# A fused image-and-text Mamba block: one state in four gets u times B from TensorE as a turned u times a diagonal of B, and the queues get another order

## The chip, the cores and the metric

The kernel runs on one core of a Trainium2 chip. A core has five engines with a queue each: PE (TensorE, matrix products into PSUM), DVE (VectorE), ACT (ScalarE), POOL (GpSimd) and SP (SyncE), which issues nearly all DMAs here. Each queue runs in order, and engines meet through semaphores. The metric is the device time of one execution in microseconds; the median of three runs of the kernel before is 1729.16 (1728.2 to 1730.28).

## The reference

64 images of 96x96 become 36 patch tokens each, a class token goes in front and 77 text tokens behind: 114 tokens of 256 values. A layer norm and a selective state-space layer follow, then a layer norm and a shared feed-forward part, and for 512 chosen rows a part with 8 experts. The state-space layer takes most of the time:

```
delta = softplus(dt @ W_dt + b_dt)
dA  = exp(delta[..., None] * A)
dBu = delta[..., None] * Bm[:, :, None, :] * xc[..., None]
h = dA_t * h + dBu_t
y = einsum('bdn,bn->bd', h, C_t)
```

There are 512 channels d and 16 states n; h runs over the 114 tokens of each sequence. With u = delta * xc the summand of the recurrence is u[d, t] * B[n, t].

## The kernel before

Sequences are taken in pairs, 32 groups of 228 columns (tokens). The main loop makes one step for each group, and a step also does the earlier layers for the next groups and the later layers for the groups before. In a step the 512 channels and 16 states are cut into 16 units (k = 0 to 15, UNITS): a unit holds one block of 128 channels (c = k // 4) and, on its 128 partitions, 4 states of 32 channels each, with four blocks of 32 channels side by side: 4 x 228 = 912 columns.

A unit goes through five instructions. POOL makes u times B into a ring of 8 SBUF buffers (`dbu`, line 1646, reading `bbc`, the rows of B spread over partitions). ACT writes the decays exp(delta * A) into one of two PSUM slots of 912 columns (`exps`, line 1010, four instructions). DVE runs the recurrence as a scan over both (`scan`, line 1307). The product with C is made by DVE from the slot (`times_c`, line 1316), or, for the six units of `ON_POOL`, by POOL (line 1654); for these the scan writes to the ring buffer. PE adds up the states with four matmuls on 32 rows of output each (`reduce_states`, line 711, after the skip product of line 708 at each first state of a block). The slot of a unit is free when its product, or for a unit of `ON_POOL` its scan, is done; only then may ACT fill it for the unit after next.

The order of each engine's queue is written out in the bodies of its block, as a loop over k with conditions. On ACT the window (`window`) stands behind unit 1: SiLU of the convolved x for the next group and of z, with a table load before and after (lines 1041, 1047, 1132). On PE the z projection of the next group (`proj_z`, line 610) stands behind unit 13 and the convolution (line 661) behind units 9 and 12. delta of the next group comes out behind unit 7 on DVE (line 1357), after three softplus instructions of ACT (lines 1058 to 1066); u follows on POOL (line 1667). Both go through DRAM to be spread over partitions.

## Time and profile before

| | |
|---|---|
| median of 3 runs | 1729.16 us |
| span of the profiled execution | 1726.7 us (2.5 us less than the median) |
| busy: PE, DVE, ACT, POOL | 1480.7, 1555.7, 1331.9, 1564.6 us |
| one step in the middle of the run | 49.2 us |
| mean granted TensorE clock | 0.947 of 2.4 GHz |

Busy times are those of a whole execution and hide that each stage has its own limit. PE's busy time counts a matmul until its modelled end, so back-to-back matmuls overlap; an fp32 matmul shows as two records (line 711: 4 matmuls, 8 records), a transpose as one. In the timelines the text in brackets is idle time of that engine just before the instruction, and what ended it.

### The profile page before, as it was taken

To read this page: it belongs to the slowest core of one execution; us is meant where nothing else is said; L and a number is where in the kernel's file an instruction comes from. 1 tells how busy PE (TensorE), PEld (TensorE's weight loads), DVE (VectorE), ACT (ScalarE), POOL (GpSimd) and SP (SyncE) were. 2 spreads that over 40 slices of the span, in tenths; PEclk is the share of its full clock that TensorE was granted. 3 is DMA by queue.
4 is the path that set the end of the run, shared out by engine and by line. 5 is a ranking of instruction groups with operands and counts; after the bars stand their busy time and mean duration, and the time that the engine had idled before them with its cause. 6 is when DMAs were issued, how large, how long until landed. Compare 5 with 4: busy or idle time off the path is not lost.

```text
span 1726.7 us, 28038 instructions
## 1 busy us (share of the span) xinstructions
PE 1480.7 (86%) x9868; PEld 1065.4 (62%) x9868; DVE 1555.7 (90%) x1389; ACT 1331.9 (77%) x3100; POOL 1564.6 (91%) x782
## 2 busy tenths in 40 slices
PE   7778898889888988898889889888889898977688
PEld 7555666666666666666666666666666666654355
DVE  2599999999999999999999999999999999999944
ACT  2577788888888888888888888888888888886644
POOL 0699999999999999999999999999999999999814
PEclk9888999999999999999999999999999999997899
DMA  4667755555656655656666555566665555656110
GB/s 141 138 135 180 163 130 123 122 131 132 145 129 146 132 123 122 131 130 146 129 146 135 122 125 126 130 146 129 145 138 121 125 126 129 142 119 141 36 34 15
DMA packets 194430, 218.47 MB, mean 127 GB/s; under 512 B 94011, under 2 KB 184773, under 8 KB 193778
## 3 DMA queue, kind: packets, MB, share of 16 engines
q1 hardware_dynamic: 193522, 215.51, 56.6%
q8 instruction: 78, 1.28, 0.3%
q0 software_dynamic: 576, 1.17, 0.3%
q14 instruction: 62, 0.51, 0.1%
q10 hardware_dynamic: 192, 0.01, 0.0%
HBM read 169.92 MB, written 47.09 MB: 126 GB/s over the span
## 4 chain that ended last, share of the span: by engine, by line
DVE 41%; ACT 18%; issue 16%; PE 13%; POOL 10%; DMA 2%; SPq 0%; DVEq 0%; ACTq 0%; POOLq 0%
DVE psum L1307 20%; DVE xr L1307 16%; ACT psum L1010 6%; POOL xr L1646 6%; POOL xr L1654 3%; PE psum L610 3%; DVE xr L1316 3%; ACT L1132 2%; PE psum L697 2%; PE psum L782 2%; ACT L1041 2%; ACT soft L1062 2%; ACT soft L1066 2%; ACT soft L1058 2%; PE psum L783 1%
## 5 line engine op out<-in xcount | busy, mean ns | idle before, releaser
L1646 POOL TENSOR_TENSOR xr<-u,bbc 128x912 f32<-128x912 f32 x512 | 1075.5, 2133 | 14.3 <-DMA u<-u_scratch 13.9
L1010 ACT ACTIVATE psum<-delta,a_neg 128x228 f32<-128x228 f32 x2048 | 805.9, 441 | 221.6 <-DVE xr L1316 191.2
L1307 DVE TENSOR_TENSOR_SCAN psum<-psum,xr 128x912 f32<-128x912 f32 x320 | 656.2, 2051 | 68.5 <-ACT psum L1010 59.8
L1654 POOL TENSOR_TENSOR xr<-xr,cbc 128x912 f32<-128x912 f32 x192 | 409.2, 2131 | 31.9 <-DVE xr L1307 28.5
L1307 DVE TENSOR_TENSOR_SCAN xr<-psum,xr 128x912 f32<-128x912 f32 x192 | 392.3, 2043 | 0.0
L1316 DVE TENSOR_TENSOR xr<-psum,cbc 128x912 f32<-128x912 f32 x320 | 353.7, 1105 | 11.1
L711 PE MATMUL psum<-xr,fold 128*32 128x228 f32 x4096 | 295.1, 385 | 50.6 <-POOL xr L1654 26.7
L610 PE MATMUL psum<-xh,win 128*128 128x228 f32 x1024 | 222.7, 367 | 61.8 <-ACT xs L1041 33.4
L610 PEld LDWEIGHTS psum<-xh,win 128*128 128x128 f32 x1024 | 192.1, 193 | 91.7 <-ACT xs L1041 44.0
L661 PE MATMUL psum<-xi,conv_d 128*128 128x228 f32 x1024 | 210.9, 358 | 0.0
L711 PEld LDWEIGHTS psum<-xr,fold 128*32 128x32 f32 x4096 | 96.9, 112 | 178.1 <-issue 79.4
L661 PEld LDWEIGHTS psum<-xi,conv_d 128*128 128x128 f32 x1024 | 190.2, 188 | 16.2 <-issue 11.7
L730 PE MATMUL psum<-wout,y 128*114 128x256 f32 x512 | 134.8, 411 | 0.0
L708 PE MATMUL psum<-xs,skip_w 128*128 128x228 f32 x256 | 83.2, 408 | 30.0 <-DVE y L1324 30.0
L730 PEld LDWEIGHTS psum<-wout,y 128*114 128x114 f32 x512 | 97.4, 200 | 18.8
L625 PE MATMUL psum<-xp,tokw 128*128 128x72 f32 x768 | 92.3, 278 | 8.4 <-DMA xp<-x_patches 8.4
L625 PEld LDWEIGHTS psum<-xp,tokw 128*128 128x128 f32 x768 | 92.8, 196 | 10.0 <-DMA xp<-x_patches 8.9
L1667 POOL TENSOR_TENSOR u<-delta,xs 128x912 f32<-128x912 f32 x31 | 65.9, 2125 | 18.4 <-issue 12.0
L708 PEld LDWEIGHTS psum<-xs,skip_w 128*128 128x128 f32 x256 | 40.9, 194 | 67.1 <-DVE y L1324 44.4
L697 PE MATMUL psum<-dbl,wdt 17*128 17x228 f32 x256 | 58.7, 369 | 22.2 <-ACT ob L1122 21.8
L697 PEld LDWEIGHTS psum<-dbl,wdt 17*128 17x128 f32 x256 | 46.0, 189 | 36.6 <-issue 34.0
L756 PE MATMUL psum<-x2t,w 128*128 128x228 f32 x256 | 58.8, 374 | 1.9
(204 smaller groups left out, 1574.7 us busy)
## 6 DMA issues: line engine op xcount, KB each, us to landing
delta<-delta_scratch SPq DMA_DIRECT2D x256, 228.0 KB, 6.5
u<-u_scratch SPq DMA_DIRECT2D x256, 228.0 KB, 4.2
bbc<-bc_scratch SPq DMA_DIRECT2D x128, 114.0 KB, 2.6
u_scratch<-u SPq DMA_DIRECT2D x64, 228.0 KB, 4.9
cbc<-bc_scratch SPq DMA_DIRECT2D x128, 114.0 KB, 2.7
delta_scratch<-delta SPq DMA_DIRECT2D x64, 226.0 KB, 5.7
out<-ob SPq DMA_DIRECT2D x32, 228.0 KB
h_scratch<-h SPq DMA_DIRECT2D x31, 228.0 KB
```

Source lines behind the costliest of these rows:

```text
L610: mm = pe.matmul(bank[:, c], win[:, k, at + c * P:at + (c + 1) * P], xh[:, p, k], start=(k == 0), stop=(k == DC - 1))
L625: mm = pe.matmul(tok_ps[:, c, g % 2:g % 2 + count].rearrange("p h t -> p (h t)"), tokw[:, k, c * P:(c + 1) * P], xp[:, k, g % 2:g % 2 + co ...
L661: mm = pe.matmul(conv_bank(half)[:, c].rearrange("p (s t) -> p s t", s=SEQ), conv_d[:, at, t], xi[:, at, :, t:t + T], start=(t == 0), stop ...
L697: mm = pe.matmul(dt_bank(half)[:, c], wdt[32:33 + R, (2 * half + c) * P:(2 * half + c + 1) * P], dbl[32:33 + R, :], start=True, stop=True)
L708: pe.matmul(y_ps, skip_w[:, c], xs[:, i % 2, c], start=True, stop=False)
L711: mm = pe.matmul(y_ps[j * DQ:(j + 1) * DQ], fold[:], xr[:, k % XRING, j], start=False, stop=(n == NI - 1))
L730: mm = pe.matmul(h2_ps[:, s], y[:, g % 2, c, s * T:(s + 1) * T], wout[:, c], start=False, stop=(c == CH - 1))
L1010: ins = nc.scalar.activation(slot(k)[:, j * TOK:(j + 1) * TOK], delta4[:, c // 2, j, c % 2], ACT.Exp, scale=a_neg[:, c, j, n:n + 1])
L1307: nc.vector.tensor_tensor_scan(x if k in ON_POOL else slot(k), slot(k), x, 0.0, ALU.mult, ALU.add).then_inc(scan_done, 1)
L1316: nc.vector.tensor_tensor(xr[:, k % XRING], slot(k).rearrange("p (j t) -> p j t", j=J), cbc[:, p, k % NI].unsqueeze(1).to_broadcast([P, J, ...
L1646: nc.gpsimd.tensor_tensor(xr[:, k % XRING], u4[:, c // 2, :, c % 2], bbc[:, p, n].unsqueeze(1).to_broadcast([P, J, TOK]), ALU.mult).then_i ...
L1654: nc.gpsimd.tensor_tensor(xr[:, k % XRING], xr[:, k % XRING], cbc[:, p, k % NI].unsqueeze(1).to_broadcast([P, J, TOK]), ALU.mult).then_inc ...
```

## The change

In units 0, 4, 8 and 12 (`turned(k)`: state 0 of each four) the summand u times B comes from PE and no longer from POOL. PE turns u of the whole group (`turn_u`, eight transposes into the PSUM space of slot 0), ACT copies it to SBUF (`ut_copy`), and for each turned unit `times_b` multiplies turned u with a diagonal matrix that has B of one state and sequence on its diagonal; the result goes into the unit's PSUM slot, where the decays used to be, and the decays of that unit go to the ring buffer in SBUF. The diagonal matrices lie in DRAM as zeros; two DMAs a step write B into the diagonal word by word (`diag_keep`), one reads the whole matrix back (`diag_load`). POOL makes the products with C of eight units, DVE of eight. The queues' orders are written out anew, instruction by instruction. `e1` shares the space of `win` and is loaded near the end; `est` shares that of `ut`.

```diff
-ON_POOL = (1, 3, 8, 10, 12, 14)
+TURNED = 0
+ON_POOL = ((0, 3, 5, 7, 8, 10, 12, 13),)
...
+            ut_ps = flat[0:T, 0:CH * SEQ * P].rearrange("p (c s d) -> p c s d", c=CH, s=SEQ)
...
+            def slot_free(e, i, k):
+
+                back = (k - SLOTS) % UNITS
+                step = i if k >= SLOTS else i - 1
+                if step < 0 or back in on_pool(step):
+                    need(e, scan_done, UNITS * i + k - SLOTS + 1)
+                else:
+                    e.wait_ge(c_dve, dve_products(step, back) + 1)
...
+                    def diag_keep(g):
+
+                        need(sp, diag_in, 16 * (g - 1))
+                        if g == 0:
+                            sp.wait_ge(diag_out, 32)
+                        lines = diag_scratch[g % 2].rearrange("(t x) -> t x", t=T)[:, 0:SEQ * NQ * T]
+                        spots = lines.rearrange("t (s q z) -> q s t z", s=SEQ, q=NQ)[:, :, :, 0]
+                        for s in range(SEQ):
+                            sp.dma_start(spots[:, s], dbl[TURNED:NS:NI, s * T:(s + 1) * T],
+                                         allow_slow_non_contiguous=True).then_inc(diag_out, 16)
+
+                    def diag_load(g):
+                        sp.wait_ge(diag_out, 16 * SEQ * (g + 2))
+                        need(sp, bu_mm, CH * (g - 1))
+                        sp.dma_start(diag[0:T, g % 2].rearrange("p s q t -> p (s q t)"), diag_flat(g)).then_inc(diag_in, 16)
...
                             sp.wait_ge(dbl_ev, i + 2)
                             sp.dma_start(bc_scratch[p], dbl[0:2 * NS, :]).then_inc(bc_out, 16)
+                            diag_keep(i + 1)
 
                             sp.wait_ge(bc_out, 16 * (i + 2))
-                            rows_out(bbc, p, 0, b_in)
+                            b_rows_out(p)
                             rows_out(cbc, p, NS, c_in)
+                            diag_load(i + 1)
...
+                    def turn_u(g):
+
+                        pe.wait_ge(u_done, 2 * g + 2)
+                        slot_free(pe, g, TURNED)
+                        for c in range(CH):
+                            for s in range(SEQ):
+                                mm = pe.transpose(ut_ps[:, c, s], u[:, c, s * T:(s + 1) * T], ident[:])
+                        mm.then_inc(ut_mm, 1)
+
+                    def times_b(i, k):
+
+                        c = k // NI
+                        pe.wait_ge(ut_ev, i + 1)
+                        pe.wait_ge(diag_in, 16 * (i + 1))
+                        slot_free(pe, i, k)
+                        lo = (k % SLOTS) * 1024
+                        for j in range(J):
+                            for s in range(SEQ):
+                                a = lo + j * TOK + s * T
+                                cut = min(T, 512 - a % 512)
+                                for x, z in ((0, cut), (cut, T)):
+                                    for q in range(NQ):
+                                        if x < z:
+                                            mm = pe.matmul(flat[q * DQ:(q + 1) * DQ, a + x:a + z], ut[0:T, c, s, j * DQ:(j + 1) * DQ],
+                                                           diag[0:T, i % 2, s, q, x:z], start=True, stop=True)
+                        mm.then_inc(bu_mm, 1)
...
+                        if runs(i + 1):
+                            turn_u(i + 1)
+                        if runs(i + 2):
+                            convolve(i + 2, 1)
+                        if runs(i):
+                            reduce_states(i, 12)
+                        if runs(i + 1):
+                            times_b(i + 1, 0)
...
+                        if turned(k):
+                            need(act, red_mm, v - XRING + 1)
+                            to = xr[:, k % XRING].rearrange("p j t -> p (j t)")
                         else:
-                            need(act, c_dve, N_DVE * step + ON_DVE.index(back) + 1)
+                            slot_free(act, i, k)
+                            to = slot(k)
...
+                    def ut_copy(g):
+                        act.wait_ge(ut_mm, g + 1)
+                        need(act, bu_mm, CH * g)
+                        nc.scalar.activation(ut[0:T], ut_ps, ACT.Copy).then_inc(ut_ev, 1)
...
-                        dve.wait_ge(dbu_done, v + 1)
                         x = xr[:, k % XRING].rearrange("p j t -> p (j t)")
-                        nc.vector.tensor_tensor_scan(x if k in ON_POOL else slot(k), slot(k), x, 0.0,
+                        decay, added = slot(k), x
+                        if turned(k):
+                            dve.wait_ge(bu_mm, CH * i + k // NI + 1)
+                            decay, added = x, slot(k)
+                        else:
+                            dve.wait_ge(dbu_done, made(i, k) + 1)
+                        nc.vector.tensor_tensor_scan(x if k in on_pool(i) else slot(k), decay, added, 0.0,
                                                      ALU.mult, ALU.add).then_inc(scan_done, 1)
...
+                        if turned(k):
+                            return
                         need(pool, red_mm, v - XRING + 1)
```

On PE the end of a step and the start of the next read so before, from the feed-forward input (L756) over the convolution (L661), the state reductions (L711, eight for two units) and the z projections (L610):

```order
L756 MATMUL psum<-x2t,w 128x228 x4
L661 MATMUL psum<-xi,conv_d 128x228 x8
L711 MATMUL psum<-xr,fold 32x228 x8
L708 MATMUL psum<-xs,skip_w 128x228
L711 MATMUL psum<-xr,fold 32x228 x4
L661 MATMUL psum<-xi,conv_d 128x228 x8
L711 MATMUL psum<-xr,fold 32x228 x4
L610 MATMUL psum<-xh,win 128x228 x8
L711 MATMUL psum<-xr,fold 32x228 x8
L708 MATMUL psum<-xs,skip_w 128x228
L711 MATMUL psum<-xr,fold 32x228 x4
L767 MATMUL psum<-vv,cent_h 128x228
```

Now the same place reads as follows, with turn_u at L797, times_b at L814, the reductions at L787, the convolution at L737 and the z projections at L686:

```order
L787 MATMUL psum<-xr,fold 32x228 x8
L797 MATMUL psum<-ident,u 114x128 x8
L737 MATMUL psum<-xi,conv_d 128x228 x8
L784 MATMUL psum<-xs,skip_w 128x228
L787 MATMUL psum<-xr,fold 32x228 x4
L814 MATMUL psum<-diag,ut 32x114 x16
L814 MATMUL psum<-diag,ut 32x56 x4
L814 MATMUL psum<-diag,ut 32x58 x4
L814 MATMUL psum<-diag,ut 32x114 x12
L787 MATMUL psum<-xr,fold 32x228 x8
L686 MATMUL psum<-xh,win 128x228 x8
L787 MATMUL psum<-xr,fold 32x228 x4
```

turn_u of the next group stands behind the reductions of units 10 and 11 and waits for the product of unit 14; times_b of the next group's unit 0 stands ahead of the reductions of units 13 and 14 and of the z projections.

On DVE the step's border reads so before, from the scan of unit 14 to that of unit 2 (scans are L1307 and print as SCALAR_TENSOR_TENSOR here, products with C are L1316):

```order
L1307 SCALAR_TENSOR_TENSOR xr<-psum,xr 128x912
L1307 SCALAR_TENSOR_TENSOR psum<-psum,xr 128x912
L1316 TENSOR_TENSOR xr<-psum,cbc 128x912
L1378 SCALAR_TENSOR_TENSOR gate<-psum,b,gate 128x228
L1385 SCALAR_TENSOR_TENSOR vv<-psum,b,gate 128x228
L1363 BN_STATS st<-h 114x6 x2
L1307 SCALAR_TENSOR_TENSOR psum<-psum,xr 128x912
L1316 TENSOR_TENSOR xr<-psum,cbc 128x912
L1372 BN_AGGR mv<-st 114x2 x2
L1307 SCALAR_TENSOR_TENSOR xr<-psum,xr 128x912
L1324 TENSOR_TENSOR y<-psum,sz 128x456
L1307 SCALAR_TENSOR_TENSOR psum<-psum,xr 128x912
```

Now, from the product of unit 14 on (scans are L1473, products L1482; the scan that reads `xr,psum` is that of the turned unit 0):

```order
L1482 TENSOR_TENSOR xr<-psum,cbc 128x912
L1473 SCALAR_TENSOR_TENSOR psum<-psum,xr 128x912
L1548 SCALAR_TENSOR_TENSOR gate<-psum,b,gate 128x228
L1482 TENSOR_TENSOR xr<-psum,cbc 128x912
L1557 SCALAR_TENSOR_TENSOR vv<-psum,b,gate 128x228
L1529 BN_STATS st<-h 114x6 x2
L1473 SCALAR_TENSOR_TENSOR xr<-xr,psum 128x912
L1538 BN_AGGR mv<-st 114x2 x2
L1473 SCALAR_TENSOR_TENSOR psum<-psum,xr 128x912
L1490 TENSOR_TENSOR y<-psum,sz 128x456
L1482 TENSOR_TENSOR xr<-psum,cbc 128x912
L1473 SCALAR_TENSOR_TENSOR psum<-psum,xr 128x912
```

Units 1 and 14 have their product on DVE now and unit 0 on POOL, and the first half of the gate stands ahead of the product of unit 15.

## Rows read from the trace of the kernel before

**Rows 1.** The page's first part, busy time of each engine
```profile
PE 1480.7 (86%) x9868; PEld 1065.4 (62%) x9868; DVE 1555.7 (90%) x1389; ACT 1331.9 (77%) x3100; POOL 1564.6 (91%) x782
```

**Rows 2.** Stretches: length; PE, PEld, DVE, ACT, POOL busy; PEclk; DMA; GB/s
```profile
871.06:874.48 3.42, 3.42 (x22) 1.76 (x20) 3.39 (x4) 3.36 (x6) 3.42 (x2) 0.50 0.08 28
...
849.30:898.50 49.20, 43.57 (x301) 31.25 (x301) 47.04 (x39) 40.54 (x96) 47.95 (x24) 0.97 0.62 134
```

**Rows 3.** Timeline of DVE, scan 2 to scan 2: start us, us, instruction
```profile
808.07 2.07 DVE L1307 TENSOR_TENSOR_SCAN psum<-psum,xr 128x912 f32<-128x912 f32 x1 [1.78 <-ACT psum L1010]
...
847.13 1.11 DVE L1316 TENSOR_TENSOR xr<-psum,cbc 128x912 f32<-128x912 f32 x1
848.16 0.45 DVE L1378 SCALAR_TENSOR_TENSOR gate<-psum,b,gate 128x228 f32<-128x228 f32 x1
848.64 0.46 DVE L1385 SCALAR_TENSOR_TENSOR vv<-psum,b,gate 128x228 f32<-128x228 f32 x1
...
849.67 2.05 DVE L1307 TENSOR_TENSOR_SCAN psum<-psum,xr 128x912 f32<-128x912 f32 x1
...
851.82 1.11 DVE L1316 TENSOR_TENSOR xr<-psum,cbc 128x912 f32<-128x912 f32 x1
...
853.00 2.02 DVE L1307 TENSOR_TENSOR_SCAN xr<-psum,xr 128x912 f32<-128x912 f32 x1
854.95 0.60 DVE L1324 TENSOR_TENSOR y<-psum,sz 128x456 f32<-128x456 f32 x1
857.33 2.06 DVE L1307 TENSOR_TENSOR_SCAN psum<-psum,xr 128x912 f32<-128x912 f32 x1 [1.78 <-ACT psum L1010]
```

**Rows 4.** Timeline of ACT around the window
```profile
848.28 1.58 ACT L1010 ACTIVATE psum<-delta,a_neg 128x228 f32<-128x228 f32 x4 [1.46 <-DVE xr L1316]
...
853.86 0.55 ACT L1047 ACTIVATE sz<-psum 128x456 f32<-128x456 f32 x1 [0.77 <-PE psum L610]
854.43 1.28 ACT L1132 ACT_TABLE_LOAD   x1
855.72 1.58 ACT L1010 ACTIVATE psum<-delta,a_neg 128x228 f32<-128x228 f32 x4
```

**Rows 5.** Timeline of PE, end of a step and start of the next
```profile
844.75 3.35 PE L661 MATMUL psum<-xi,conv_d 128*128 128x228 f32 x16
848.04 0.59 PE L711 MATMUL psum<-xr,fold 128*32 128x228 f32 x8
...
852.01 1.81 PE L610 MATMUL psum<-xh,win 128*128 128x228 f32 x8 [1.05 <-ACT xs L1041]
...
853.75 0.98 PE L711 MATMUL psum<-xr,fold 128*32 128x228 f32 x16
...
855.61 0.65 PE L708 MATMUL psum<-xs,skip_w 128*128 128x228 f32 x2 [0.88 <-DVE y L1324]
```

**Rows 6.** The page's fifth part, u times B: xcount | busy, mean ns
```profile
L1646 POOL TENSOR_TENSOR xr<-u,bbc 128x912 f32<-128x912 f32 x512 | 1075.5, 2133 | 14.3 <-DMA u<-u_scratch 13.9
```

**Rows 7.** Timeline of PE and ACT, transposes and a copy out of PSUM
```profile
826.20 0.58 PE L743 MATMUL psum<-ident,h2n 114*128 114x114 f32 x4 [1.77 <-DVE delta L1357]
...
1700.01 1.04 PE L949 MATMUL psum<-ident,xr 128*128 128x128 f32 x8
...
1701.08 1.11 ACT L1252 ACTIVATE xr<-psum,selg 128x1024 f32<-128x1024 f32 x1 [1.28 <-PE psum L949]
```

**Rows 8.** Timeline of ACT and DVE around delta
```profile
821.53 0.93 ACT L1058 ACTIVATE soft<-psum 128x912 f32<-128x912 f32 x1
...
824.36 1.56 ACT L1010 ACTIVATE psum<-delta,a_neg 128x228 f32<-128x228 f32 x4
...
824.96 1.09 DVE L1357 SCALAR_TENSOR_TENSOR delta<-psum,soft 128x912 f32<-128x912 f32 x1
```

**Rows 9.** Timeline of SP's queue between the rows of dbl and those of delta
```profile
813.34 0.31 SPq L537 DMA_DIRECT2D bc_scratch<-dbl  x1
...
826.08 1.25 SPq L465 DMA_DIRECT2D delta_scratch<-delta  x2
```

More of the change, by code:

```diff
@@ L49, in fusion_kernel, with on_pool, pool_products, dve_products @@
     E = gate_w.shape[2] - 1
-    ON_DVE = tuple(k for k in range(UNITS) if k not in ON_POOL)
-    N_DVE, N_POOL = len(ON_DVE), len(ON_POOL)
+    def on_pool(g):
+        return ON_POOL[g % len(ON_POOL)]
+    def pool_products(g, k):
+        return sum(len(on_pool(a)) for a in range(g)) + sum(x < k for x in on_pool(g))
+    def dve_products(g, k):
+        return UNITS * g + k - pool_products(g, k)
+    ALL_DVE = dve_products(GROUPS, 0)
+    MADE = NI - 1
+    def turned(k):
+        return k % NI == TURNED
+    def made(g, k):
+        return MADE * CH * g + MADE * (k // NI) + (k % NI) - (k % NI > TURNED)
+    ALL_MADE = made(GROUPS, 0)
     bc_scratch = nc.dram_tensor("bc_scratch", (2, 2 * NS, TOK), F32, kind="Internal").ap()
@@ L805, in before_first @@
                             convolve(1, half)
+                        turn_u(0)
+                        times_b(0, TURNED)
                         for half in range(2):
@@ L919, in hidden @@
                     def hidden(m, j):
+                        if m == 0 and j == 0:
+                            pe.wait_ge(e1_in, 16)
                         if m >= 1:
@@ new lines, in body @@
+                        if runs(i):
+                            ut_copy(i)
+                            exps(i, p, 0)
+                            exps(i, p, 1)
+                        window(i, p)
+                        if runs(i):
+                            exps(i, p, 2)
+                            exps(i, p, 3)
+                        if runs(i - 2):
+                            ln2_rstd(i - 2)
+                        if runs(i - 3):
+                            v_square(i - 3)
+                            ln3_rstd(i - 3)
@@ new lines, in body @@
+                        if runs(i):
+                            scan(i, 0)
+                        if runs(i - 2):
+                            ln2_ready(i - 2)
+                            ln2_moments(i - 2)
+                        if runs(i):
+                            scan(i, 1)
+                        if runs(i - 1):
+                            y_out(i - 1, q, 1)
+                        if runs(i):
+                            times_c(i, p, 1)
+                            scan(i, 2)
+                            times_c(i, p, 2)
+                            scan(i, 3)
@@ new lines, in body @@
+                        if runs(i + 2):
+                            image_tokens(i + 2)
+                        if runs(i):
+                            scan(i, 4)
+                        if runs(i - 3):
+                            v_norm(i - 3)
+                        if runs(i):
+                            times_c(i, p, 4)
+                            scan(i, 5)
+                            scan(i, 6)
+                            times_c(i, p, 6)
+                            scan(i, 7)
@@ new lines, in body @@
+                        if runs(i + 1):
+                            delta_out(i + 1)
+                        if runs(i):
+                            scan(i, 8)
+                            scan(i, 9)
+                            times_c(i, p, 9)
+                        if runs(i + 2):
+                            normalize(i + 2, p)
+                        if runs(i):
+                            scan(i, 10)
+                            y_out(i, p, 0)
+                            scan(i, 11)
+                            times_c(i, p, 11)
+                            scan(i, 12)
+                            scan(i, 13)
+                            scan(i, 14)
+                            times_c(i, p, 14)
+                            scan(i, 15)
```

335 lines of the change are left out of this document (197 added, 138 removed).

## The prediction

> **What bounds the kernel now.** I read the page's table of engines first: DVE and POOL are busy 90 and 91 per cent of the span, PE 86, ACT 77 [rows 1]. Four engines near their end call for the view by stretches, cut at the step: in one step of 49.2 us, from the middle of the run, PE works 43.57 us, DVE 47.04, ACT 40.54, POOL 47.95 [rows 2]. The step itself is the distance between two scans of unit 2, 857.33 - 808.07 = 49.26 us, and there DVE has its only idle time, 1.78 us, ended by ACT [rows 3]. So a step is 47.48 us of DVE work and 1.78 us of one wait. The timeline of ACT tells what the wait is: when the product of unit 15 is done (848.24), ACT writes the exponentials of unit 1, goes through the window (table load, four SiLU of x, two of z, table load), and only then writes those of unit 2 [rows 4]. Inside that window SiLU of z waits for PE, whose z projection runs from 852.01 to 853.82 [rows 5]. From the end of product 15 to scan 2 that makes 857.33 - 848.24 = 9.1 us, while DVE has 7.3 us of work of its own. DVE and POOL both sit near 48 us, PE less than 6 us below the step: whatever takes work from the first two and gives it to PE has little room.
>
> **What the change does to each engine in a step.** Three sums, from the step of rows 2.
>
> POOL loses 4 of its 16 products u times B and takes 8 instead of 6 products with C. One such product is 2.13 us [rows 6], so 2 x 2.13 = 4.3 us leave, 47.95 - 4.3 = 43.7. POOL stops being a bound.
>
> DVE loses 2 of its 10 products with C. One costs 1.03 us from its start to the next start (847.13 to 848.16) [rows 3]: 47.48 - 2.06 = 45.4 us of work. The scans of the turned units read their factor in SBUF and their summand in PSUM; no row shows that way round. The scans of before that write SBUF and those that write PSUM are 2.02 and 2.05 us [rows 3], so I take 2.05, with 0.1 us either way.
>
> PE gains four times_b and one turn_u. turn_u is eight transposes of 128 columns: the row of eight such takes 1.04 us [rows 7]. times_b has 36 matmuls a unit, nine pieces of four that go to the four 32-column strips of the array, seven of 114 columns and two that make 114 together. The trace has this form with 228 columns, in the reduction at line 711: one unit (four matmuls, 8 records) takes 0.59 us and two in a row 0.98 [rows 5], so a further group of four costs 0.39 us. Four transposes of 114 columns take 0.58 us where a single 228-column matmul has 0.65 for its two records [rows 5, 7], so time goes with columns: a piece of 114 columns is half of 0.39. Lower bound: 8 x 0.195 = 1.56 us for a unit. Upper bound: each of nine pieces costs as much as one of 228 columns, 9 x 0.39 = 3.5 us. I take 1.7, near the lower end, because the transposes show short pieces going at their column count; 0.2 more passes until the last result is there. So PE gets 4 x 1.9 + 1.04 = 8.6 us: 43.57 + 8.6 = 52.2. Of today's 43.57 up to 1.7 are a stretch of 3.4 us at half clock (granted clock 0.50 from 871.06 to 874.48, that is 1.2 instead of 2.4 GHz) [rows 2], which may go away when PE has fewer gaps; that leaves 50.5. This is over 49.26 already, before any wait. The order of queues then decides how much over.
>
> ACT gains the copy of the turned u, 1.11 us by the row of a 128x1024 copy out of PSUM [rows 7], and its exponentials of turned units no longer wait for a PSUM slot. It has 8.7 us to spare in the step. The new DMAs are two of 456 single words and one of 114 rows of 3.6 KB. They go into SP's queue between the rows of dbl (813.34) and those of delta (826.08) [rows 9], with a wait for the words' landing, and delta's transfers and all that follow stand behind it. 12.7 us lie between the two today; I cost the DMAs at nothing. No row prices a DMA of single words.
>
> **The loop that sets the step after the change.** PE takes its queue in order. turn_u waits for product 14 (its result lies in slot 0, which unit 14 frees), and behind it stand the second half of the convolution, the reduction of unit 12, times_b of unit 0, the reductions of 13 and 14 and both z projections. Scan 0 needs times_b, and the window on ACT needs the projections. From the end of product 14: turn_u 1.0; convolution 844.75 to 848.04, 3.3; skip matmul and reduction of unit 12, 1.1; times_b 1.7, result 0.2 later, so scan 0 can start at 7.2 us [rows 5, 7]. DVE has until then scan 15 (2.05), the gate (848.16 to 848.64, 0.48), product 15 (1.03), the second half of the gate and the statistics (848.64 to 849.67, 1.03): 4.6 us [rows 3]. It stands for 2.6 us at scan 0. PE goes on: two reductions 0.9 (to 7.9), projections 2 x 1.74, result at 11.5; SiLU of z 0.57, table load 1.28, exponentials of unit 2 1.58 [rows 4, 5]: scan 2 starts 14.9 us after product 14. DVE's own work in that stretch is 4.6, scan 0 (2.0), moments with a product (851.82 to 853.00, 1.18), scan 1 (853.00 to 854.95, 1.95) and y (0.55), together 10.3 us [rows 3]. So 4.6 us of idle time stand where 1.78 stood.
>
> The other three times_b wait for product 2, product 6 and scan 10, each two or three DVE instructions ahead of the scan that needs it; queued behind them on PE are the centring, the variance with the output projection, and the second x projection. These waits I put at under 1 us a step, in the forecast's own range.
>
> The rest of the step, scan 2 to product 14, is 45.4 - 10.3 = 35.1 us of DVE work. One more wait is in it. Today delta comes out at 824.96, 16.9 us after scan 2, just behind the softplus on ACT (821.53 to 824.36) [rows 8]. DVE now gets there one product sooner, at 15.9, while the softplus ends at 16.3 as before (PE has a times_b more ahead of the projection it waits for): 0.4 to 0.5 us. And the exponentials of unit 8, 1.58 us, stand behind the softplus; product 7 (1.03 us) lay over them and is on POOL now: 0.6 us more. Together 1.1. The step is 14.9 + 35.1 + 1.1 = 51.1 us by DVE's loop, and PE's own sum is 50.5. I take 50.9: 1.6 us more than today, in 31 steps 50 us. The first step waits until turn_u, the copy and times_b are through, about 4 us later; the last step has no next one to prepare for and runs at DVE's 45.4, 4 us sooner. The profiled execution has a span of 1726.7 [rows 1] where the median is 1729.16; the 2.5 us around it stay. 1729 + 50 = 1779 us.
>
> **A rule of the skill against the change.** The reduction's second group of eight records takes 0.39 us, 49 ns each, so nothing here shows how short a record can get [rows 5]. The Trainium skill (TensorE: Matmul & The Clock Gate, section "Wait — 56ns, not 53.3ns?") says that matmuls never start closer than about 25 ns however few columns they have, and 62 ns when their decoding is left to the sequencer. By 25 ns the 72 records of a times_b would take 1.8 us, an estimate from that page, and the forecast would stand; by 62 ns 4.5 us, which the 49 ns of the row already contradict.
>
> **The rivals.**
> - *PE keeps up (faster).* If PE gets through turn_u, times_b and the projections early enough that scan 0 does not wait and the window closes 9.1 us after product 15 as today, DVE idles there for 9.1 less its own work, 7.3 less the half of the gate that now goes ahead of product 15 (0.48): 9.1 - 6.8 = 2.3 us. The step is 45.4 + 2.3 = 47.7 us; 1729 - 31 x 1.5 = 1682 us. For it: DVE and POOL have really less to do. Against it: PE's 50.5 us of work. It decides at the loop from product 14 to scan 2: with the 35.1 behind it, 14.1 us of loop and softplus wait would give today's step, and I count 14.9 + 1.1.
> - *Even.* The softplus wait doesn't arise and the loop is 0.6 us shorter: 14.3 + 35.1 = 49.4, 1729 + 4 = 1733 us.
> - *A floor for each record.* times_b costs nearer to 3.5 us than to 1.7. Each of the four adds 1.8 us to PE, 7.2 a step, all of it on the bound: 50.9 + 7.2 = 58.1, 1729 + 31 x 8.8 = 2000 us; a third of the way there gives 1850.
> - *The change takes no load off, since its DMAs come late:* if the words land after more than the 12.7 us, delta and u go out late and ACT or POOL wait for them at the next step; each us over is one us a step, and 3 us over would give 1779 + 31 x 3 = 1872 us.
>
> **How the numbers follow.** Forecast 1779 us with 0.55 (its own range 1745 to 1815: the loop 1 us shorter or longer). PE keeps up 0.16; even 0.09; floor 0.13; late DMAs 0.07. The run-to-run spread is about 0.2 per cent, 3.5 us, so only outside 1725.7 to 1732.6 is a change told from none. Faster 0.17, same 0.08, slower 0.75. The range of 8 in 10 goes from 1710, inside the faster case (about 0.12 lie below), to 1840, about a third of the way to the floor (0.08 above).
>
> **What would show it.** In the profile after: PE busy near 50 us a step with hardly any half clock; POOL at about 44; a times_b of 1.7 to 1.9 us in the timeline of PE; DVE idle before scan 0 (released by PE) and before scan 2 (by ACT), together about 4.6 us a step; delta_out with a small wait for ACT. Wrong is the forecast if times_b takes over 2.2 us, if DVE never waits for PE at scan 0, or if PE stands idle for several us a step while the step is still longer than 49.3.

## The result and the profile after

The changed kernel takes 1755.02 us (median of 4 runs, 1752.6 to 1762.21), the kernel before 1728.84 beside it (4 runs, 1728.2 to 1730.28): a ratio of 1.0156, 95% interval 1.0135 to 1.0178. It is slower, by 26 us where 50 were forecast.

The page's table of engines and, below it, one steady step in the view by stretches (PE, weight load, DVE, ACT, POOL busy; granted clock; DMA share; GB/s):

```profile
PE 1643.5 (94%) x19340; PEld 1289.4 (73%) x19340; DVE 1490.7 (85%) x1325; ACT 1353.9 (77%) x3132; POOL 1436.1 (82%) x719
```
```profile
818.48:868.73 50.25, 48.52 (x604) 38.38 (x597) 45.08 (x37) 41.06 (x97) 43.97 (x21) 1.00 0.62 136
```

Against [rows 1, 2] PE has risen by 5 us a step, DVE and POOL have fallen by 2 and 4, and the clock is at its upper level (1.00) all through the step. The timeline of DVE shows where its freed time went (start, duration, idle time before and what ended it):

```profile
810.46 1.11 DVE L1482 TENSOR_TENSOR xr<-psum,cbc 128x912 f32<-128x912 f32 x1
...
815.17 0.74 DVE L1529 BATCH_NORM_STATS2 st<-h 114x6 f32<-114x256 f32 x2
818.48 2.05 DVE L1473 TENSOR_TENSOR_SCAN xr<-xr,psum 128x912 f32<-128x912 f32 x1 [2.56 <-PE psum L814]
...
822.98 0.63 DVE L1490 TENSOR_TENSOR y<-psum,sz 128x456 f32<-128x456 f32 x1 [0.37 <-PE psum L787]
823.53 1.10 DVE L1482 TENSOR_TENSOR xr<-psum,cbc 128x912 f32<-128x912 f32 x1
825.90 2.07 DVE L1473 TENSOR_TENSOR_SCAN psum<-psum,xr 128x912 f32<-128x912 f32 x1 [1.27 <-ACT psum L1147]
...
842.09 1.11 DVE L1523 SCALAR_TENSOR_TENSOR delta<-psum,soft 128x912 f32<-128x912 f32 x1 [0.47 <-issue]
843.53 2.05 DVE L1473 TENSOR_TENSOR_SCAN xr<-xr,psum 128x912 f32<-128x912 f32 x1 [0.33 <-ACT xr L1147]
...
868.73 2.05 DVE L1473 TENSOR_TENSOR_SCAN xr<-xr,psum 128x912 f32<-128x912 f32 x1 [2.56 <-PE psum L814]
```

From scan 0 to scan 0 are 868.73 - 818.48 = 50.25 us. Where [rows 3] had one wait of 1.78 us, there are now 2.56 for times_b of unit 0 (L814), 0.37 for reduction 15 (ahead of y<-psum,sz, called y_out below), 1.27 for the exponentials of unit 2, and 0.8 around delta: 5.0 us. So the time that DVE was freed of, and more, is now idle time. PE in the same place, to be held against [rows 5]:

```profile
811.72 1.06 PE L797 MATMUL psum<-ident,u 128*114 128x128 f32 x8
812.61 3.25 PE L737 MATMUL psum<-xi,conv_d 128*128 128x228 f32 x16
815.70 0.55 PE L784 MATMUL psum<-xs,skip_w 128*128 128x228 f32 x2
816.18 0.59 PE L787 MATMUL psum<-xr,fold 128*32 128x228 f32 x8
816.59 1.75 PE L814 MATMUL psum<-diag,ut 114*32 114x114 f32 x72
818.16 0.96 PE L787 MATMUL psum<-xr,fold 128*32 128x228 f32 x16
819.04 3.35 PE L686 MATMUL psum<-xh,win 128*128 128x228 f32 x16
822.32 0.59 PE L787 MATMUL psum<-xr,fold 128*32 128x228 f32 x8
```

No row here waits: from turn_u on, PE goes from one piece of work to the next without a gap, and DVE and ACT wait for what stands late in that queue. ACT shows the far end of the loop, where [rows 4] had one wait for PE, of 0.77:

```profile
812.81 1.02 ACT L1154 ACTIVATE ut<-psum 114x1024 f32<-114x1024 f32 x1 [0.77 <-PE psum L797]
...
820.89 0.55 ACT L1189 ACTIVATE sz<-psum 128x456 f32<-128x456 f32 x1 [1.31 <-PE psum L686]
822.43 0.55 ACT L1189 ACTIVATE sz<-psum 128x456 f32<-128x456 f32 x1 [0.99 <-PE psum L686]
823.00 1.28 ACT L1275 ACT_TABLE_LOAD   x1
```

From the end of product 14 (810.46 + 1.11 = 811.57) to scan 2 (825.90) the loop takes 14.33 us.

### The profile page after: what moved, and what is told of

Its sections match the earlier page's. It is cut to its first block, busy times and chain, and to the rows that moved or that the text cites. A ratio compares the mean times of both kernels' runs of the same rounds, so it can differ in the third digit from the quotient of the medians.

```text
span 1754.6 us, 47205 instructions
## 1 busy us (share of the span) xinstructions
PE 1643.5 (94%) x19340; PEld 1289.4 (73%) x19340; DVE 1490.7 (85%) x1325; ACT 1353.9 (77%) x3132; POOL 1436.1 (82%) x719
## 4 chain that ended last, share of the span: by engine, by line
PE 56%; POOL 14%; DVE 13%; ACT 8%; issue 6%; DMA 2%; SPq 1%; DVEq 0%; POOLq 0%; ACTq 0%
PE psum L737 11%; POOL xr L1847 9%; PE psum L787 9%; DVE xr L1473 7%; PE psum L814 7%; PE psum L686 7%; PE psum L833 6%; PE psum L711 3%; POOL xr L1855 3%; ACT psum L1147 3%; PE psum L859 2%; DVE psum L1473 2%; PE psum L784 2%; PE psum L797 2%; PE psum L830 2%
## 5 line engine op out<-in xcount | busy, mean ns | idle before, releaser
L1847 POOL TENSOR_TENSOR xr<-u,bbc 128x912 f32<-128x912 f32 x384 | 808.9, 2135 | 59.9 <-PE psum L787 46.2
L1147 ACT ACTIVATE psum<-delta,a_neg 128x228 f32<-128x228 f32 x1536 | 600.9, 438 | 141.1 <-DVE xr L1482 106.1
L1855 POOL TENSOR_TENSOR xr<-xr,cbc 128x912 f32<-128x912 f32 x256 | 540.0, 2126 | 152.6 <-DVE xr L1473 151.3
L1473 DVE TENSOR_TENSOR_SCAN psum<-psum,xr 128x912 f32<-128x912 f32 x224 | 458.4, 2046 | 43.3 <-ACT psum L1147 40.0
L1473 DVE TENSOR_TENSOR_SCAN xr<-psum,xr 128x912 f32<-128x912 f32 x160 | 327.0, 2044 | 0.0
L1482 DVE TENSOR_TENSOR xr<-psum,cbc 128x912 f32<-128x912 f32 x256 | 282.5, 1103 | 5.7
L1473 DVE TENSOR_TENSOR_SCAN xr<-xr,psum 128x912 f32<-128x912 f32 x96 | 196.8, 2050 | 105.5 <-PE psum L814 96.3
L787 PE MATMUL psum<-xr,fold 128*32 128x228 f32 x4096 | 257.4, 363 | 7.5 <-POOL xr L1855 7.5
L814 PE MATMUL psum<-diag,ut 114*32 114x114 f32 (+2 forms) x9216 | 237.5, 258 | 25.5 <-DVE xr L1482 22.7
L814 PEld LDWEIGHTS psum<-diag,ut 114*32 114x32 f32 x9216 | 214.5, 113 | 56.2 <-issue 47.5
L686 PE MATMUL psum<-xh,win 128*128 128x228 f32 x1024 | 223.6, 367 | 4.4 <-DVE xh L1503 2.6
L686 PEld LDWEIGHTS psum<-xh,win 128*128 128x128 f32 x1024 | 187.0, 190 | 35.5 <-issue 18.0
L737 PE MATMUL psum<-xi,conv_d 128*128 128x228 f32 x1024 | 210.8, 357 | 0.0
L1147 ACT ACTIVATE xr<-delta,a_neg 128x228 f32<-128x228 f32 x512 | 204.8, 471 | 6.6 <-DMA delta<-delta_scratch 6.2
L737 PEld LDWEIGHTS psum<-xi,conv_d 128*128 128x128 f32 x1024 | 188.0, 188 | 15.3 <-issue 10.9
L787 PEld LDWEIGHTS psum<-xr,fold 128*32 128x32 f32 x4096 | 106.7, 109 | 107.0 <-issue 56.6
```

What stands on the lines that cost most here:

```text
L686: mm = pe.matmul(bank[:, c], win[:, k, at + c * P:at + (c + 1) * P], xh[:, p, k], start=(k == 0), stop=(k == DC - 1))
L737: mm = pe.matmul(conv_bank(half)[:, c].rearrange("p (s t) -> p s t", s=SEQ), conv_d[:, at, t], xi[:, at, :, t:t + T], start=(t == 0), stop ...
L787: mm = pe.matmul(y_ps[j * DQ:(j + 1) * DQ], fold[:], xr[:, k % XRING, j], start=False, stop=(n == NI - 1))
L814: mm = pe.matmul(flat[q * DQ:(q + 1) * DQ, a + x:a + z], ut[0:T, c, s, j * DQ:(j + 1) * DQ], diag[0:T, i % 2, s, q, x:z], start=True, stop ...
L1147: ins = nc.scalar.activation(to[:, j * TOK:(j + 1) * TOK], delta4[:, c // 2, j, c % 2], ACT.Exp, scale=a_neg[:, c, j, n:n + 1])
L1473: nc.vector.tensor_tensor_scan(x if k in on_pool(i) else slot(k), decay, added, 0.0, ALU.mult, ALU.add).then_inc(scan_done, 1)
```

## The experiments

Step lengths below are distances between the rows of DVE's timeline that write delta (delta_out): 49.26 us before and 50.25 after in nearly all steps.

**The order on PE (e1_conv_last).** The second half of the convolution goes behind times_b of unit 0, so that scan 0 need not wait for it.

```
-                        if runs(i + 2):
-                            convolve(i + 2, 1)
                         if runs(i):
                             reduce_states(i, 12)
                         if runs(i + 1):
                             times_b(i + 1, 0)
+                        if runs(i + 2):
+                            convolve(i + 2, 1)
```

> One edit to the changed kernel: on PE, times_b of the next group's unit 0 goes ahead of the second half of the convolution instead of behind it. Theory (a loop from product 14 through turn_u, the convolution, times_b, the z projections and the window on ACT sets the step): the wait at scan 0, 2.56 us, goes, because times_b is done about 4.1 us after product 14 and DVE arrives at 4.3; the wait before scan 2 grows by as much, because the same PE work still stands ahead of the z projections. Step 50.2 to 50.7 us, time 1753 to 1770. Rival (the wait at scan 0 is itself the price): step 50.25 - 2.5 = 47.7 us, time about 1677.

Measured 1778.54 us, ratio 1.0294 [1.0274, 1.0313]; step 51.0. DVE's timeline and then PE's:

```profile
834.92 0.63 DVE L1490 TENSOR_TENSOR y<-psum,sz 128x456 f32<-128x456 f32 x1 [3.68 <-PE psum L787]
837.84 2.06 DVE L1473 TENSOR_TENSOR_SCAN psum<-psum,xr 128x912 f32<-128x912 f32 x1 [1.27 <-ACT psum L1147]
```

```profile
822.92 1.06 PE L797 MATMUL psum<-ident,u 128*114 128x128 f32 x8
...
825.09 1.78 PE L814 MATMUL psum<-diag,ut 114*32 114x114 f32 x72 [0.20 <-ACT ut L1154]
826.79 3.35 PE L737 MATMUL psum<-xi,conv_d 128*128 128x228 f32 x16
830.08 0.98 PE L787 MATMUL psum<-xr,fold 128*32 128x228 f32 x16
...
834.26 0.59 PE L787 MATMUL psum<-xr,fold 128*32 128x228 f32 x8
```

Scan 0 has no wait left, as expected. But scan 2's wait, which I expected to grow, is still 1.27; y_out has the time, behind reduction 15. 2.56 + 0.37 + 1.27 = 4.2 us have become 3.68 + 1.27 = 4.95, and that difference is PE's: from turn_u to the end of the z projections it takes 834.26 - 822.92 = 11.34 us, in the changed kernel 822.32 - 811.72 = 10.60. 0.20 of it are a wait for the copy of the turned u, and the convolution takes 3.29 in this place where it took 3.09. Faster, as the rival had it, is refuted; the time is 8 us over the top of what I expected.

**The size of times_b (e2_half_b).** The loop over sequences in times_b ends after the first, so half of each product is left out.

```
-                            for s in range(SEQ):
+                            for s in range(SEQ - 1):
```

> times_b leaves out the second sequence of each pair: 18 or 20 instead of 36 matmuls a unit, so half of the summand is not made. Theory (loop): of the four times_b only that of unit 0 lies in the loop; it gets 0.8 us shorter, step 49.3 to 49.6 us, time 1725 to 1735. Rival (PE's sum of work is the bound, wherever the matmuls stand): PE loses 4 x 0.8 = 3.2 us a step and the step follows until DVE binds, 47.4 us, time about 1667.

Measured 1745.98 us, ratio 1.011 [1.0083, 1.0137]. DVE's timeline in the middle:

```profile
816.82 2.05 DVE L1473 TENSOR_TENSOR_SCAN xr<-xr,psum 128x912 f32<-128x912 f32 x1 [1.78 <-PE psum L814]
...
821.32 0.63 DVE L1490 TENSOR_TENSOR y<-psum,sz 128x456 f32<-128x456 f32 x1 [0.37 <-PE psum L787]
...
824.24 2.07 DVE L1473 TENSOR_TENSOR_SCAN psum<-psum,xr 128x912 f32<-128x912 f32 x1 [1.27 <-ACT psum L1147]
```

Half of the 1.57 us of a times_b is 0.78. The wait at scan 0 falls by 2.56 - 1.78 = 0.78, the other two stay to the hundredth, and the step falls by 0.78, to 49.47. Four such halves are out of the step, but only the one in the loop counts: PE's sum of work does not set the step. The total is 11 us over what I expected. In the profiled execution (1740.13 us) seven early steps took 51.16 (7 x 1.69 = 11.8 us), with DVE waiting in other places; what puts the kernel into that rhythm for a while is open, and so is what the other executions, up to 1751.74 us, did.

**The single-word DMAs (e3_no_words).** The words of dbl are written to the diagonals for the first two groups only, and the waits for them are changed to fit.

```
...
-                            diag_keep(i + 1)
+                            if i + 1 < 2:
+                                diag_keep(i + 1)
...
```

> The two DMAs of single words are left out from the third group on (the diagonals keep the B of the first two groups); the matrix is still read back each step. Theory (loop on PE): the DMAs are off the path, time 1755 within 0.3 per cent, 1750 to 1760. Rival (the words, or the wait of SP for them, delay delta and u, or the DMA engines): time falls by some us, below 1748.

Measured 1758.12 us, ratio 1.016 [1.013, 1.0189], the step 50.26: as with them. The DMAs of 912 words a step cost nothing that shows.

**Unit 0 back on POOL (e4_three).** Only units 4, 8 and 12 are turned. POOL makes unit 0, its four rows of B come by four DMAs more, and no times_b stands in the loop. turn_u stays there with six transposes, and the exponentials of unit 0, which go to slot 0 again, wait for the copy of the turned u.

```
-        return k % NI == TURNED
+        return k % NI == TURNED and k >= NI
...
-                        if runs(i + 1):
-                            times_b(i + 1, 0)
...
```

> Only units 4, 8 and 12 are turned: unit 0 gets its summand from POOL again, from one more row of B; six transposes instead of eight, a copy of 768 columns, three times_b. Theory (loop): times_b of unit 0 (1.57 us from start to start) and two transposes (0.25) leave the loop from product 14 to scan 2, the wait at scan 0 goes, about 2.4 us stay before scan 2. Step 48.2 to 48.7 us, time 1692 to 1710, faster than before the change. Rival (POOL or ACT becomes late: POOL has 46.1 us of work): step near 49.3 or more, no gain over before, 1729 or above.

Measured 1730.77 us, ratio 1.0015 [0.9995, 1.0035]: 24 us better than four, yet 20 over the top of what I expected and where the rival had it. ACT does become late, as the rival said, but for a transfer and not for its own or POOL's work. Steps went from 48.0 to 52.1. What was late in the long ones is in ACT's timeline:

```profile
947.94 0.81 ACT L1159 ACTIVATE ut<-psum 114x768 f32<-114x768 f32 x1 [0.55 <-PE psum L803]
951.04 3.08 ACT L1152 ACTIVATE psum<-delta,a_neg 128x228 f32<-128x228 f32 x8 [2.29 <-DMA delta<-delta_scratch]
```

The exponentials of units 0 and 1, which stand ahead of the window, wait for delta's way through DRAM. A wait that four turned units had covered is now the last one.

**The z projections earlier, four turned (e8_four_z).** Both z projections go ahead of reductions 13 and 14.

```
-                        if runs(i):
-                            reduce_states(i, 13)
-                            reduce_states(i, 14)
                         if runs(i + 1):
                             proj_z(i + 1, 1 - p, 0)
                             proj_z(i + 1, 1 - p, 1)
                         if runs(i):
+                            reduce_states(i, 13)
+                            reduce_states(i, 14)
                             reduce_states(i, 15)
```

> The changed kernel (four turned) with the two z projections ahead of reductions 13 and 14 on TensorE, nothing else. Theory, the loop from product 14 over turn_u, the convolution, the product of unit 0, the z projections, the SiLU of z and the exponentials of unit 2 to scan 2 sets the step: taking the two reductions (0.9 us) out from ahead of the z projections takes 0.9 to 1.1 us off a step of 50.25, 1720 to 1735 us. Rival, TensorE is full (48.5 of 50.25 us busy) and what is moved ahead there only makes the rest late: 1745 to 1760.

Measured 1733.96 us, ratio 1.0026 [1.0016, 1.0036], mostly steps of 49.55, that is 0.70 less where 0.9 to 1.1 were expected. DVE's timeline in one of them:

```profile
807.24 2.05 DVE L1472 TENSOR_TENSOR_SCAN xr<-xr,psum 128x912 f32<-128x912 f32 x1 [2.56 <-PE psum L814]
...
811.74 0.63 DVE L1489 TENSOR_TENSOR y<-psum,sz 128x456 f32<-128x456 f32 x1 [0.36 <-PE psum L787]
...
813.89 2.07 DVE L1472 TENSOR_TENSOR_SCAN psum<-psum,xr 128x912 f32<-128x912 f32 x1 [0.50 <-ACT psum L1146]
...
819.64 2.06 DVE L1472 TENSOR_TENSOR_SCAN psum<-xr,psum 128x912 f32<-128x912 f32 x1 [0.38 <-ACT xr L1146]
```

Scan 2's wait fell by 0.77 and y_out's stayed; the wait of 0.47 ahead of delta_out is gone, and scan 4 has a new one of 0.38. PE does the same work as in the changed kernel, in another order, and 21 of the 26 us of loss are gone. The rival is refuted: the loop sets the step.

**Delta ahead of u (e6_three_delta), and reduction 15 ahead of the z projections too (e7_three_both).** Three turned; two lines of SP change places, and in the second run a line of PE moves as well.

```
+                        spread_delta(g, half)
                         spread_u(g, half)
-                        spread_delta(g, half)
 ...
                             reduce_states(i, 14)
+                            reduce_states(i, 15)
                         if runs(i + 1):
                             proj_z(i + 1, 1 - p, 0)
                             proj_z(i + 1, 1 - p, 1)
-                        if runs(i):
-                            reduce_states(i, 15)
```

> Units 4, 8 and 12 turned (unit 0 made by GpSimd as before), and SP issues the spreading of delta's half ahead of that of u's half instead of behind it. Theory: with three turned units no product on TensorE stands between product 14 and scan 0 any more, and the next thing late is delta: in the three-turned run the exponentials of units 0 and 1 waited 0.9 to 2.3 us a step for delta's copy from DRAM, and the table load, both SiLUs and the exponentials of unit 2, for which scan 2 waits, stand behind them on ScalarE. With delta's transfers issued 2.6 us earlier that wait goes: steps of 47.2 to 48 us in place of 48 to 52, 1660 to 1690 us in all. Rival 1, reduction 15 behind the z projections on TensorE is what holds the step (y_out waited 1.9 to 3.1 us for it): nothing moves, 1720 to 1735. Rival 2, u is then late for GpSimd's first product of a step, which waited for nothing there: slower, 1735 to 1760.

> The kernel just described (three turned, delta's transfers ahead of u's) with reductions 13, 14 and 15 all ahead of the two z projections on TensorE instead of 15 behind them. Theory: scan 2 waits for the exponentials behind ScalarE's window, and y_out's wait for reduction 15 only lies in front of that wait; z projections start 0.45 us later but the second waits for the SiLU of x anyway. So y_out's wait goes and scan 2's grows by as much: within 0.5% of the kernel without this edit (1655 to 1695). Rival: y_out's wait is on the path, and then this is 20 to 45 us faster than the kernel without this edit.

Measured 1755.63 us, ratio 1.0165 [1.0135, 1.0196], and 1780.01, ratio 1.029 [1.0271, 1.0309]. Both of my theories fell; the second rival of the first run holds, and the second run, 24 us slower than the first, is where neither of its expectations was. POOL's timeline, its line of the page for those products, and PE's timeline, all of the first:

```profile
853.55 2.13 POOL L1852 TENSOR_TENSOR xr<-u,b 128x912 f32<-128x912 f32 x1 [3.76 <-issue]
```
```profile
L1852 POOL TENSOR_TENSOR xr<-u,b 128x912 f32<-128x912 f32 x32 | 68.0, 2125 | 127.4 <-issue 113.4
```
```profile
857.80 0.98 PE L793 MATMUL psum<-xr,fold 128*32 128x228 f32 x16 [1.25 <-POOL xr L1860]
```

POOL stands 3.76 us before the step's first product with u, and 113.4 us in the whole run (11.9 in e4_three); the trace names no releaser there, but u's loads are what the edit put off. Behind that product in POOL's queue is a product with C for which PE then waits. With reduction 15 ahead as well, the z projections stand behind that wait too, and scan 2 waits 2.41 us for ACT. So either order has one transfer late. I took it that both together take too long; the next runs test that.

**The diagonals' load later (e9_three_diag, e10_three_diag_r15).** u first again; the load of the diagonals (406 KB) leaves its place ahead of the stores of delta and u and goes behind the spreading of their first halves. The second run has reduction 15 ahead of the z projections too.

```
                         rows_out(cbc, p, NS, c_in)
-                            diag_load(i + 1)
 ...
                         spread_half(i + 1, 0)
+                            diag_load(i + 1)
```

> Three units turned, u's half spread ahead of delta's as in the first three-turned kernel; the load of the diagonals (406 KB) is issued behind the spreading of the first halves of u and delta instead of ahead of the stores of delta and u. Theory: transfers are late in the three-turned kernels, because the diagonals' 406 KB lie in the DMA engines' queues ahead of delta's and u's way through DRAM (their stores take 7 to 8 us to land, their loads 5.7 and 7.9 us); at the 150 GB/s that the engines moved, 406 KB are 2.7 us. So delta lands 2 to 3 us earlier, the exponentials of unit 0 wait for it by under 0.3 us, u is not late for GpSimd, steps are 47.3 to 48.5 us: 1665 to 1700 us. Rival, the engines share their bandwidth so that the diagonals only meet other transfers (the second halves) and those are late instead: 1715 to 1745.

> The kernel just described with reduction 15 ahead of the z projections on TensorE too. Theory: where u is not late, GpSimd has product 15 done when TensorE comes to it, y_out does not wait for reduction 15 and what is left is scan 2's wait for ScalarE: within 0.5% of the kernel without this edit, or up to 15 us faster. Rival: GpSimd's product 15 is still late, TensorE stands before it and the z projections, SiLU and scan 2 with it, as where delta was put first: 20 to 35 us slower than the kernel without this edit.

Measured 1716.58 us, ratio 0.9928 [0.9909, 0.9947]: faster than both kernels, but 17 us over the theory's range and just inside the rival's. 11 of 31 steps are 48.46, within what the theory has, and 17 times delta is still late; which of the two it is the next runs tell. With reduction 15 ahead 1731.71, ratio 1.0026 [1.0008, 1.0045], between the two expectations: y_out's wait (1.2 to 1.9 us) goes, and scan 2's grows by as much or more, from 1.27 to 3.1 us, behind later z projections.

**The diagonals' load last (e12_three_diag_last), and the z projections first (e13_three_diag_last_z).** The load goes behind the second halves; the second run has the PE edit of e8_four_z in addition.

```
                         spread_half(i + 1, 0)
-                            diag_load(i + 1)
 ...
                         spread_half(i + 1, 1)
+                            diag_load(i + 1)
```

> Three units turned, the load of the diagonals behind the spreading of the second halves of u and delta as well (in the run before it stood behind the first halves only). There the step was 48.46 us where delta was in time, and the steps above that summed to some 20 us, with 17 waits of the exponentials of unit 0 for delta. Theory, the diagonals' transfer still lies over delta's first half while that lands: those waits go, all steps near 48.5 us, 1695 to 1710 us. Rival, the diagonals are now too late for the product of unit 4 (TensorE gets to it 9 us after the issue) and TensorE and scan 4 wait for them: 1720 to 1760. Rival 2, it is not the diagonals that make delta late in those steps: 1712 to 1720, as before this edit.

> The kernel just described with both z projections ahead of reductions 13 and 14 on TensorE, which took 0.7 us off the step with four turned units. Theory: with three, the second z projection waits for the SiLU of x (850.4 in the stretch read), and so can be done only 0.25 us earlier than now, while reduction 15 and y_out come 0.6 us later, inside scan 2's wait: 0 to 0.25 us a step, 0 to 8 us in all. Rival, the loop is as long on TensorE as with four turned units, and it takes 0.7 us off a step: 18 to 25 us.

Measured 1703.39 us, ratio 0.9846 [0.983, 0.9862], and 1708.04, ratio 0.9882 [0.9863, 0.9902]. The waits for delta's copy over the whole run (us, times), in e4_three, e9_three_diag and e12_three_diag_last:

```profile
  ACT psum L1152: 32.9, 28
```
```profile
  ACT psum L1152: 17.6, 17
```
```profile
  ACT psum L1152: 4.7, 11
```

The time falls with them, 1730.8, 1716.6, 1703.4: 14 us for 15 us of waits, then 13 for 13. That is the theory of this run, and it settles the run before: it was still the diagonals that made delta late. About half of the steps (15 of 31) are now 48.46, 0.8 under before; all 31 together are 5.5 us over that. One of them by stretches, and DVE's timeline at a border:

```profile
820.82:869.28 48.46, 46.72 (x526) 36.43 (x522) 44.93 (x37) 41.04 (x96) 45.94 (x23) 1.00 0.63 143
```
```profile
843.94 0.63 DVE L1495 TENSOR_TENSOR y<-psum,sz 128x456 f32<-128x456 f32 x1 [1.28 <-PE psum L793]
844.49 1.10 DVE L1487 TENSOR_TENSOR xr<-psum,cbc 128x912 f32<-128x912 f32 x1
846.86 2.07 DVE L1478 TENSOR_TENSOR_SCAN psum<-psum,xr 128x912 f32<-128x912 f32 x1 [1.27 <-ACT psum L1152]
```

The window is still the last thing. With the z projections first the steady step is 48.50, no gain, and the total is 5 us more where 0 to 8 less were expected: y_out waits 2.45 us and scan 2 still 0.50. The rival, 18 to 25 us less, is refuted. In the profiled executions the spans are 2.9 us apart, and so are the waits for delta's copy (7.6 us in 12 against 4.7 in 11); where the rest of the 5 us in the median comes from was not followed.

**The same move with four turned (e11_four_z_diag).** e8_four_z with the SP edit of e9_three_diag.

> Four units turned, z projections ahead of reductions 13 and 14, and the diagonals' load moved on SP behind the spreading of the first halves of u and delta (which gave 14 us with three turned units). Theory: a transfer is worth what the wait for it is worth; with four turned units no steady step waits for delta (scan 0 waits for the product of unit 0, 2.56 us), so the move gives nothing: 1728 to 1737 us, within 0.3% of the 1734 without it. Rival 1, less traffic ahead of u and delta is worth as much here: 1715 to 1725. Rival 2, the diagonals, now issued some 9 us ahead of the product of unit 0, land too late for it: 1740 to 1800.

Measured 1753.98 us, ratio 1.0154 [1.0137, 1.0171]: not the theory but the second rival. DVE's waits for times_b, nearly all at unit 0, in e8_four_z and in this kernel (us, times); then PE's waits at times_b that no releaser is named for (us, times, longest), of which e8_four_z has none, and one of them with SP's issue of the load ahead of it:

```profile
  DVE xr L1472: 97.0, 33
```
```profile
  DVE xr L1472: 110.1, 33
```
```profile
PE psum L814 <- issue: 8.4, 13, 1.5
```
```profile
948.17 0.28 SPq L567 DMA_DIRECT2D diag<-diag_scratch  x1
```
```profile
960.48 1.78 PE L814 MATMUL psum<-diag,ut 114*32 114x114 f32 x72 [1.36 <-issue]
```

The spans of the profiled executions are 1743.1 and 1732.0, 11 us apart, and DVE's waits for times_b differ by 13. Here the load is issued 12.3 us ahead of the product, and PE stands idle before it; of what the product waits for, the diagonals are what the edit put off. With unit 0 turned they are needed at the border itself; with three units they are needed at unit 4. That the rest of the 20 us in the median has the same cause was not seen in a trace.

## Why the prediction was right, and where its size was off

The path, the waits and what ends them came as forecast; the loss was put at 50 us, about twice the 26 measured.

- *POOL and DVE.* Forecast 43.7 and 45.4 us of work a step, measured 43.97 and 45.08. The scan with its factor in SBUF and its summand in PSUM takes 2.05, the value chosen.
- *The loop.* It runs through the steps named. Scan 0 was put at 7.2 us after product 14 (its pieces add up to 7.3, a slip that the later sums do not carry) and starts at 6.91 (818.48 - 811.57); the second projection at 11.5, measured 822.43 - 811.57 = 10.9 where SiLU takes it; scan 2 at 14.9, measured 14.33. Idle time of DVE there was put at 4.6 and is 4.2. e2_half_b shows that the loop sets the step (0.78 out of it are 0.78 of the step), e8_four_z that PE's order in it decides.
- *The term that was mis-sized* is PE's time for the pieces of the loop. I took them from [rows 5]. In the loop of after, start to start, the same pieces are shorter: turn_u 0.89 for 1.0, convolution 3.09 for 3.3, skip and reduction 0.89 for 1.1, times_b 1.57 for 1.7, z projections 3.28 for 3.48. Together 0.86 us; the loop came out 0.57 shorter, since two gaps that the sum didn't have take 0.26 back (0.15 ahead of turn_u, 0.11 between the projections and SiLU). times_b is at the lower bound of 1.56 that the prediction had worked out, and turn_u had been put at the whole length of a row, until its modelled end. The other three have one reason, which the timelines of PE show. A convolution of before, one of after, each with the row behind it:

```profile
839.56 3.25 PE L661 MATMUL psum<-xi,conv_d 128*128 128x228 f32 x16
842.74 0.98 PE L711 MATMUL psum<-xr,fold 128*32 128x228 f32 x16
```
```profile
805.81 3.35 PE L737 MATMUL psum<-xi,conv_d 128*128 128x228 f32 x16
809.00 1.70 PE L859 MATMUL psum<-x2t,w 128*128 128x228 f32 x8
```

The first has reductions, which write 32 rows each, on one side of it (behind) and takes 3.18 us to the next start; the second has them ahead, and takes 3.19. The one of [rows 5] has them on both sides, 3.29; that in the loop of after, between turn_u and the skip product, on neither, 3.09. So each neighbour that writes 32 rows instead of 128 costs the convolution 0.1 us. Skip and reduction, and the two projections taken one by one, have two such borders more in [rows 5] than in the loop, 0.2 us each: with the convolution's 0.2 that is 0.6 of the 0.86 us. The prices were right for their places in the queue of before; the change moved them to other places.
- *Softplus and delta.* Forecast 1.1 us, measured 0.47 + 0.33 = 0.8.
- *The sum.* 14.33 + 35.1 + 0.8 = 50.2. The prediction's own sum for the loop was 51.1; it took 50.9, nearer to PE's 50.5, and gave no reason for that. So +0.99 a step and not +1.6: 31 x 0.99 = 31. The spans differ by 1754.6 - 1726.7 = 27.9. By the delta_out rows the first four steps with what lies ahead of them add 1.2 us to that (4 forecast), and the last step with what lies behind it takes 4.5 off (4 forecast). That the 4 came out is luck: 3.2 of the 4.5 lie behind the last scan, for which the forecast had nothing, and what got shorter there was not followed.
- *PE's own sum* was put at 50.5 and is 48.52, with hardly any half clock, as said. The four times_b and turn_u take 7.6 us (1.57 in the loop, 1.68 to 1.78 in the other places, 0.89 for turn_u) where I counted 8.6, and the convolutions and projections are shorter too. So it did not hold that PE's work alone is over the old step of 49.26 before any wait. The order of PE's queue in the loop made the kernel slower, not the sum of its work.
- *The rivals.* "PE keeps up" failed at the point given for it (14.1 us of loop and softplus wait; it is 15.1). "Even" was near: its loop of 14.3 came true, the wait at the softplus did not go away, and 0.8 x 31 = 25 us is what separates it from the result. The floor for a record did not show: a times_b is 1.57 us for 72 records, 22 ns each on average. Its price was also too high: it put a longer times_b on the bound four times a step, and by e2_half_b only the one in the loop counts. The Trainium skill (TensorE: Matmul & The Clock Gate, section "Wait — 56ns, not 53.3ns?") has about 25 ns as the least distance of matmuls; by it the product would take 1.8 us, an estimate. The trace does not agree for matmuls on strips of 32 columns: the records of this times_b start in groups of four, as many as there are strips, and within a group 2 to 12 ns apart. Late single-word DMAs are refuted by e3_no_words. PE's timeline of after, cut to 816.58 to 816.62, has the first group:

```profile
816.59 0.28 PE L814 MATMUL psum<-diag,ut 114*32 114x114 f32 x4
```

## What to carry to other kernels

Moving work to an engine with little room is judged by the loop that crosses it, not by the engine's sum of work. Here half of the product that stood in the loop was worth its whole 0.78 us a step, and three such halves outside it nothing (e2_half_b). Three products outside the loop came out 27 us faster than before, with delta's transfers kept in time; with a fourth inside the loop the best order tried was still 5 us behind before. When one wait goes, look at which transfer is next late: here a load of 406 KB, issued early without need, was worth 27 us (e4_three to e12_three_diag_last).

## What was not expected of the hardware

- The same 16 records of a convolution took 3.09, 3.18, 3.19 or 3.29 us, none with a wait: 0.1 us for each neighbour in PE's queue that writes 32 rows instead of 128.
- The 72 records of a times_b, of at most 114 columns, pass in 1.57 us on four strips of 32 columns: they start in groups of four, 2 to 12 ns apart within a group.
- The same 406 KB issued ahead of the stores and loads of delta and u, or behind them, made ACT's waits for delta 32.9 or 4.7 us a run, a difference of 27 us in the time; yet put behind the first halves where it is needed soon it cost 20 us (e11_four_z_diag).
